# A fused attention and routing layer in fp32: the output projection as three fp32r products, two small jobs moved between engines, and a new order of work on every engine

## The reference, cut to what matters

```python
y   = clip((x * style) @ W.T * dcoef + bias, -256, 256)        # x: [128, 64, 256]
xn  = layernorm(y) * g + b
q   = l2norm(xn @ Wq) * q_scale;  k = l2norm(y @ Wk) * k_scale;  v = y @ Wv    # 16 heads of 64
att = softmax(q k^T * 8 + alibi, causal, 2 null keys) @ v       # within 64 rows
x1  = x + att @ Wout
kx  = modulated_linear(x1);  o = softmax over the heads of kx, mixed;  z = modulated_linear(o)
y2  = z + (small routed network chosen per row by two argmaxes over tile scores of z)
out = x1 + layernorm(y2) * gamma + beta
```

## Time and profile before

| | |
|---|---|
| three timed runs | 1832.64, 1833.00, 1834.09 us; median 1833.0 |
| the profiled execution | 1833.11 us, its span in the trace 1831.3 us |
| busy share of the span | PE 94%, weight loads 79%, DVE 84%, ACT 65%, POOL 64% |
| granted TensorE clock, mean | 0.97 |
| DMA | 93.63 MB moved, 51 GB/s over the span |

### The profile page before, as it was taken

The page is one execution under the profiler, slowest core; times in us unless marked ns, Lnnn a source line. Parts: engine busy times, 40 slices in busy tenths (PEclk is TensorE's granted clock), DMA queues, the critical chain, the costliest instruction groups (busy, mean ns, idle before and its releaser), DMA issues.

```text
span 1831.3 us, 62542 instructions
## 1 busy us (share of the span) xinstructions
PE 1718.0 (94%) x24806; PEld 1439.5 (79%) x24806; DVE 1545.9 (84%) x4182; ACT 1198.5 (65%) x2418; POOL 1173.0 (64%) x903
## 2 busy tenths in 40 slices
PE   4789999999999999999999999999999999999752
PEld 3568888888888888888888888888888888888641
DVE  5567799888989998889989988899899888998744
ACT  2456677777667777776676777676777777667431
POOL 0345557776777677767776777677767776776433
PEclk8899999999999999999999999999999999999875
DMA  4001222222222221222122212221222122212221
GB/s 150 15 9 29 42 49 49 49 55 59 48 46 53 59 49 45 53 59 49 45 56 56 52 42 55 56 52 45 55 54 55 43 52 55 55 47 50 55 54 44
DMA packets 341245, 93.63 MB, mean 51 GB/s; under 512 B 278289, under 2 KB 338097, under 8 KB 341169
## 3 DMA queue, kind: packets, MB, share of 16 engines
q1 hardware_dynamic: 338096, 82.04, 20.6%
q0 software_dynamic: 3072, 10.52, 2.1%
HBM read 58.95 MB, written 33.55 MB: 51 GB/s over the span
## 4 chain that ended last, share of the span: by engine, by line
PE 88%; DVE 5%; ACT 2%; POOL 1%; DMA 1%; issue 1%; SPq 1%; POOLq 0%; ACTq 0%; DVEq 0%
PE pa L442 29%; PE pb L421 7%; PE pa L449 6%; PE ps L645 6%; PE ps L487 6%; PE ps L472 5%; PE ps L479 4%; PE pc L542 4%; PE pc L622 3%; PE pa L421 3%; PE ps L557 3%; PE pb L433 3%; PE ps L489 2%; PE pb L551 2%; PE pb L428 2%; PE pc L568 1%
## 5 line engine op out<-in xcount | busy, mean ns | idle before, releaser
L1131 POOL TENSOR_TENSOR rn<-nrg,mhalf 128x16 f32<-128x16 f32 x64 | 186.6, 2915 | 160.6 <-DVE nrg L1037 160.6
L1117 POOL TENSOR_TENSOR rn<-nrg,mhalf 128x16 f32<-128x16 f32 x64 | 193.2, 3018 | 119.5 <-DVE nrg L970 119.4
L442 PE MATMUL pa<-wv,y 128*128 128x512 f32 x768 | 209.6, 409 | 0.0
L442 PE MATMUL pa<-wq,xnTs 128*128 128x512 f32 x768 | 205.1, 411 | 0.3 <-ACT kcat L703 0.3
L442 PE MATMUL pa<-wk,y 128*128 128x512 f32 x768 | 194.3, 402 | 0.9 <-ACT qn L722 0.9
L442 PEld LDWEIGHTS pa<-wq,xnTs 128*128 128x128 f32 x768 | 139.3, 191 | 51.8 <-issue 23.5
L442 PEld LDWEIGHTS pa<-wk,y 128*128 128x128 f32 x768 | 139.3, 188 | 30.9 <-ACT qn L722 1.7
L1111 POOL TENSOR_TENSOR pr<-pr,rden 128x1056 f32<-128x1056 f32 x64 | 124.7, 1949 | 54.5 <-DVE rden L943 51.8
L442 PEld LDWEIGHTS pa<-wv,y 128*128 128x128 f32 x768 | 135.4, 189 | 23.2
L1006 DVE TENSOR_TENSOR qn<-qn,rn 128x1024 f32<-128x1024 f32 x64 | 112.7, 1762 | 15.6 <-POOL rn L1117 15.0
L1092 POOL TENSOR_TENSOR kn<-kn,rn 128x1024 f32<-128x1024 f32 x64 | 122.0, 1905 | 5.0
(11 more groups left out here) (216 smaller groups left out, 4863.3 us busy)
## 6 DMA issues: line engine op xcount, KB each, us to landing
xT<-in_xT SPq DMA_DIRECT2D x64, 128.0 KB
x<-in_x SPq DMA_DIRECT2D x64, 128.0 KB, 2.1
kxdr<-kxn SPq DMA_DIRECT2D x64, 128.0 KB, 1.7
x1d<-x SPq DMA_DIRECT2D x64, 128.0 KB, 1.8
vm<-kxdr SPq DMA_DIRECT2D x128, 64.0 KB
odr<-o SPq DMA_DIRECT2D x256, 32.0 KB
on<-odr SPq DMA_DIRECT2D x64, 128.0 KB
xb<-x1d SPq DMA_DIRECT2D x64, 128.0 KB, 2.2
```

Source lines behind the costliest of these rows:

```text
L442: last = mm(bank, part(lhs(a_, k)), part(rhs(b_, k)), start=(n == 0), stop=(n == 3 * CK - 1))
L1117: g.tensor_tensor(rn[:, 0, :], nrg[:, 0, :], mhalf[:, :], ALU.pow).then_inc(S("q_rsqrt"), 1)
L1131: g.tensor_tensor(rn[:, 1, :], nrg[:, 1, :], mhalf[:, :], ALU.pow).then_inc(S("k_rsqrt"), 1)
```

## The change

1. Output projection in high and low parts. ScalarE writes the attention output from PSUM as `oH` (fp32r), VectorE writes the rest `oL = PSUM - oH`, and `Wout` is split once into `wout2`. The product is oH x high, oH x low and oL x high: 24 fp32r matmuls of 256 columns in place of 8 plain fp32 ones.
2. The layer norm `xn` of y is applied by ScalarE as scale and shift; GpSimd makes the shift (two more instructions of one column).
3. The guards of the squared norms go from VectorE to GpSimd, each with one small extra instruction ahead (`idle`).
4. The order of the blocks is new on every engine, and the ages differ: TensorE now reaches back 7 tiles (before 9), VectorE 10 (before 11), SyncE 12 (before 11).
5. Some semaphores of the set-up are merged.

```diff
+                    for r in range(HP):
+                        for a in range(2):
+                            mm(ps[:, 2, C:2 * C], part(oH[:, r, :]), part(wout2[:, a, r, :]), start=(r == 0 and a == 0), stop=False)
...
+                    for r in range(HP):
+                        mm(ps[:, 2, C:2 * C], part(oL[:, r, :]), part(wout2[:, 0, r, :]), start=False, stop=False)
...
-                    for r in range(4, HP):
-                        mm(ps[:, 2, C:2 * C], oT[:, r, :], wout[:, r, :], start=False, stop=False)
...
-                    for r in range(4):
-                        mm(ps[:, 2, C:2 * C], oT[:, r, :], wout[:, r, :], start=(r == 0), stop=False)
...
+                    fn(part(oH[:, :, :].rearrange("p r (s l) -> p s r l", s=BT)),
+                       ps[:, 0:2, :].rearrange("p s (r l) -> p s r l", l=L), ACT.Copy).then_inc(S("oT_done"), 1)
...
+                    fn(xn[:, :], pa[:, 2, C:2 * C], ACT.Identity, bias=rs[:, 1:2], scale=rs[:, 0:1]).then_inc(S("xn_done"), 1)
...
+            dve.wait_ge(S("high_parts"), 4)
+            v.tensor_tensor(part(wout2[:, 1, :, :]), wout[:, :, :], wout2[:, 0, :, :], ALU.subtract)
...
+                    v.tensor_tensor(part(oL[:, :, :].rearrange("p r (s l) -> p s r l", s=BT)),
+                                    ps[:, 0:2, :].rearrange("p s (r l) -> p s r l", l=L),
+                                    oH[:, :, :].rearrange("p r (s l) -> p s r l", s=BT), ALU.subtract).then_inc(S("oT_low"), 1)
...
-                    v.tensor_scalar(xn[:, :], pa[:, 2, C:2 * C], mv[:, 0:1], rs[:, 0:1], ALU.subtract, ALU.mult)\
-                        .then_inc(S("xn_done"), 1)
...
-                    v.tensor_scalar(nrg[:, 0, :], nrm[:, 0, :], 1e-24, None, ALU.max).then_inc(S("q_guard"), 1)
...
+                    wait(pool, "k_norm", t2)
+                    g.tensor_tensor(idle[:, 1:2], eps[:, :], eps[:, :], ALU.add)
+                    g.tensor_scalar(nrg[:, 1, :], nrm[:, 1, :], 1e-24, None, ALU.max).then_inc(S("k_guard"), 1)
```

More of the change, by code:

```diff
@@ L323, in pipeline @@
                 step(n * 2 + first + 1, 1)
-            for i in range(last, T + 11):
+            for i in range(last, T + 12):
                 step(i, i % 2)
@@ L365, in step @@
                         .then_inc(D("xT_in", p), 16)
[L366 to L372, removed]
+                if live(i, 9):
+                    if live(i, 11):
+                        wait(sp, "res_done", t11)
+                    wait_dma(sp, "x1_out", t9, 1 - p)
+                    sp.dma_start(xb[:, 1 - p, :], plain(x1d, t9)).then_inc(D("x1_back", 1 - p), 16)
                 if live(i, 5):
@@ L501, in step @@
[L501 to L525, removed]
@@ L545, in step @@
                     last.then_inc(S("mix_scores"), 1)
[L546 to L553, removed]
+                if live(i, 2):
+                    wait(pe, "v1_done", t2)
+                    wait(pe, "qn_done", t2)
+                    four(pa[:, 1, :], qn, 4).then_inc(S("qT1_mm"), 1)
+                    wait(pe, "v0_done", t2)
+                    four(pa[:, 0, :], qn, 0).then_inc(S("qT0_mm"), 1)
@@ L901, in step @@
-                if live(i, 9) or live(i, 10):
-                    if live(i, 10):
-                        wait(dve, "local_exp", t10)
-                    route = links_from(0, t9)
-                    route(v.tensor_scalar(fl[:, :, :], esc[:, :, :], 1.0, None, ALU.add))
-                    route(v.reciprocal(fl[:, :, :], fl[:, :, :]))
-                    route(v.scalar_tensor_tensor(out=over[:, :, :], in0=bc(both(fl), 2, KN), scalar=float(KN - 1),
-                                                 in1=bc(CO["steps"], 1, 2 * NC), op0=ALU.mult, op1=ALU.subtract))
+                t1, t2, t3, t4, t5, t6, t7, t8, t9, t10 = (i - n for n in range(1, 11))
@@ new lines, in step @@
+                if live(i, 3):
+                    wait(dve, "probs", t3)
+                    v.tensor_reduce(den[:, :], heads, AX, ALU.add).then_inc(S("den_done"), 1)
+                    wait(dve, "den_done", t3)
+                    v.reciprocal(rden[:, :], den[:, :]).then_inc(S("rden_done"), 1)
+                if live(i, 1):
+                    v.tensor_tensor(part(y3[:, 1 - p, 1, :, 0:BT, :]), yT[:, :, :, :], y3[:, 1 - p, 0, :, 0:BT, :], ALU.subtract)
+                    v.tensor_tensor(part(y3[:, 1 - p, 1, :, BT, :]), yT[:, :, 0, :], y3[:, 1 - p, 0, :, BT, :],
+                                    ALU.subtract).then_inc(S("yT_low"), 1)
```

748 lines of the change are left out of this document (400 added, 348 removed).

## The result

The changed kernel takes 1949.9 us in the median (four runs, 1936.7 to 1954.9) against 1833.0: the ratio is 1.063, 95% interval 1.057 to 1.068. It is slower, on the side and by the mechanism that the prediction took as the likeliest, and inside its range. The profiled execution is the fastest of the four, 1936.7 us with a span of 1934.9.

What follows compares the result with a forecast made beforehand. TensorE bounded the kernel at 26.06 us a step; VectorE would take over at 27.6. 60 x (27.6 - 26.06) = +92, +2 and -8 on 1833.1 gave 1919 us, own range 1885 to 1965, all cases 1785 to 1965.

Steps and rivals of the forecast that it cites:

- its slack of 1.5 us: VectorE's waits for TensorE in a step of the kernel before: 1.46 us, so VectorE stands 1.5 us behind.
- the third collision: Not in the prediction: GpSimd's `res` falls on VectorE's sum over the hidden units or the next instruction.
- the sum: Per-step work and waits gave a 27.6 us period; over 60 steps +92, set-up +2, pipeline end -8: +86 us.
- the ring: Not in the prediction: TensorE needs 7.9 us from `xm2` towards `om`, VectorE some 20 back; their order sets the period.
- TensorE's side: Output projection: 3.5 us of plain records removed, 24 x 0.13 = 3.1 us added; TensorE's work falls by 0.4 us.
- 256 columns are dear: Rival: 0.216 us per fp32r matmul of the projection, TensorE needs 27.7 us a step, 1930 us; chance 0.04.
- The first collision: Behind `rden`, GpSimd's 1.95 us product makes VectorE's second low part of y wait: 1.8 us lost each step.
- The second collision: GpSimd's scaling of `kn` makes VectorE's high part of y wait 1.0 us (0.7 to 1.9) each step.
- The ends: Outside the steady steps: set-up gains a VectorE subtraction, +2 us; the pipeline, a step shorter at its end, -8.
- the forecast's own range: 1885 to 1965 us, from a period of 27.2 (no waits left) to 28.3 (`kn` costing 1.9).
- The rival without collisions: GpSimd reaches `rden` late and `kn` falls behind the clipping: period 25.4 us, 1788 us; chance 0.36.
- what would show it: Signs in the new profile; the one judged: TensorE has gaps ahead of the transposes of q and of kx.

Runs made afterwards that it cites:

- e5: The changed kernel with the output projection undone: plain fp32 matmuls, no low part on VectorE; 1926.3 us.
- e8: The kernel of e7 with the output projection undone: plain fp32 matmuls, no low part on VectorE; 1856.8 us.
- e7: The kernel of e1 with the statistics of the sum and `xm2` on VectorE moved ahead of the clippings; 1908.4 us.
- e1: The changed kernel with the two subtractions for the low parts of y moved ahead of the softmax sum on VectorE; 1919.1 us.
- e4: The kernel before with the two subtractions for the low parts of y moved directly behind the reciprocal `rden`; 1910.4 us.
- e3: The changed kernel with the edits of e1 and e2 together; 1874.8 us.
- e13: The kernel of e7 with TensorE's program written out for all steps in place of a loop over pairs of steps; 1814.4 us.
- e12: The kernel of e7 without the eight matmuls of `oL` with the high part of wout, so the output lacks that product; 1806.1 us.
- e10: The kernel before with four more one-element matmuls on TensorE in each step, ahead of the output projection; 1898.2 us.
- e11: The kernel of e10 with two in place of four of the one-element matmuls in each step; 1854.7 us.
- e2: The changed kernel with `kn` scaled by GpSimd in one of its 16 heads alone; 1870.5 us.

## Why the prediction was right, and where it was off

- **Which engine bounds.** Right: VectorE took over, its slack of 1.5 us was used up. The size of the period owes something to luck: the terms below that were too small (`kn`, the third collision) and the one that was too large (`oL`) partly cancel. What the sum lacked is the ring: it asked how much work VectorE has in a step, not on which side of `xm2` and `om`. e5 shows that `oL`'s 1.14 us (1.14 measured too), which the sum counted as a loss, cost about 0.1, since TensorE needs that stretch anyway.
- **TensorE's side.** The 24 matmuls of 256 columns in a steady step of the changed kernel (timeline, PE):

```profile
1030.82 2.17 PE L495 MATMUL ps<-wout,oH 128*128 128x256 f32 x16
1032.83 0.38 PE L438 MATMUL pb<-ident,zT 128*128 128x128 f32 x2
...
1033.65 1.19 PE L512 MATMUL ps<-wout,oL 128*128 128x256 f32 x8
1034.77 0.65 PE L514 MATMUL ps<-nullw,pnT 32*64 32x256 f32 x4
```

  From start to the next start they take 2.01 + 1.12 = 3.1 us, 0.13 each, as in the sum; e8's plain ones take 3.65, so that the gain is 0.5 us a step where the sum had 0.4; the periods of e7 and e8 (26.4 and 27.0) agree. "256 columns are dear" is out. The estimate of 2.6 us that the prediction drew from the Trainium skill's figure for a weight load ("TensorE: Matmul & The Clock Gate", "LDWEIGHTS (loading the stationary operand)") is too low; the trace decides.
- **The first collision.** Right in place, instruction and size: -1.8 forecast, 2.04 - 0.28 = 1.76 measured, with GpSimd waiting 2.6 us ahead of `rden` (1.5 to 3 forecast). e1 and e4 show what it is worth: 1.4 less in the changed kernel (0.46 went to `fl`), 1.3 more in the kernel before.
- **The second collision.** Right in cause, off in place and size. Counted from k's norm as there, `kn` asks at +3.6 as forecast, and VectorE comes to `yT` 0.3 us sooner than forecast. But by the prediction's own times the two adding clippings, at about +4.0 and +4.3, already lay inside `kn`'s hold from +3.6 to +5.5. It let them pass without a reason and made only the high part wait, 1.0 us from +4.5. The first clipping starts 0.03 us behind `kn` and is held up for 1.7 (inside the 0.7 to 1.9 given). The high part is next: e1 shows it held up when the clippings come ahead of `kn`. So an operation with one input and per-partition scalars in SBUF is locked out too. The Trainium skill ("GPSIMD Engine Reference", section "8. Key points") counts among those that contend with GpSimd the operations of VectorE in a 2-port perf mode, besides those with two SBUF inputs. That would fit: the one-input high part of 256 columns takes 0.29 us where an operation with two inputs takes 0.42. No trace here names the mode.
- **The third collision** was missed: `res` on `hid` and `junk` in turn, together 0.46 us a step (their means are 422 and 450 ns, before 235 and 175).
- **The sum.** Period 27.6 forecast, 28.2 measured. Between the first and the last softmax sum the profiled execution takes 1756.0 us against 1632.7, +123.3, of which 6.9 are the two stalls; the sum had +92 for this. The ends are -19.7 where the sum had +2 and -8: the first softmax sum comes 8.2 us earlier, and the stretch behind the last is 11.5 us shorter. That the time still falls into the range beside a longer period and the stalls is in part these ends, which is luck. The result is 1950 against 1919. The lower bound of the forecast's own range doesn't follow from its period: 27.2 gives 60 x 1.14 - 6 = +62, 1895 us and not 1885.
- **Missing altogether: the stalls.** They are 7 us of the profiled execution. The median of the timed runs lies 13 us above that execution; four more stalls of 3.4 us would make that up, which is an estimate, since no profile shows such a run. Their granted clock, 0.965 to 0.967 against 0.973, is on the side of more stalls. The prediction counted records, work and waits, but not the length of the program between two jumps.
- **The rival without collisions** gave a period of 25.4 and 1788 us. e3 has 25.6 and takes 1875: its arithmetic was right to 0.2 us a step, and its conclusion wrong by 87 us, because of the stalls. Had VectorE's collisions not happened, the change would still have been slower as it stood. Without stalls and without the two large collisions (e13, `xm2` moved too) it is 1.1% faster than the kernel before. The second forecast of "what would show it", a gap ahead of the transposes of q, is wrong (there is none in the steady step), the gap ahead of kx is right.

## What to carry to other kernels

Before you place an operation of VectorE that reads two SBUF operands, or a `tensor_scalar` on SBUF, ask which GpSimd product its predecessor has just released: 0.3 us of work became 2.0 in each step. Put there what the product doesn't hold up, as `nrm`'s sum in e1 (1.20 us beside the product), and look at what meets the product's end. Ask for a saving on which side of a ring of waits it lies; 1.1 us taken from VectorE where TensorE needed the time anyway was worth 0.1. And when a change adds instructions to a loop, compare the instruction queue's packets with those of before. If they rise and TensorE waits for "issue" at the loop's start, shorten the body (e12) or write it out (e13).

## What was not expected of the hardware

- A loop of TensorE with 16 more matmuls and 16 more loads in a pass of some 775 and 775 stalls at its start, for 1.7 to 5.1 us, in some passes and not in others; with 8 and 8 more it doesn't (e10, e11). Each stall comes with nine packets on the instruction queue, and a pass without a stall has none. With a faster step more passes tend to stall (2 in the changed kernel at 28.2 us a step, 13 to 16 in e1, e3 and e7 at 25.6 to 26.8), but e2 and e10, at 26.6, have 7 and 8. Why some passes escape stays open.
- A stall costs more than TensorE's own wait, because the clock falls beside it: 4.7 to 4.8 us of idle time lengthened a step by 6.8 us in e3 and e7, where TensorE has next to no slack, and by 5.5 in e1. In the changed kernel, where TensorE waits for `xm2` in each step anyway, it was 3.4, with 3.4 us at 1.2 GHz.
- The same program written out reads 3.29 MB of instructions, where e7 with its 13 stalls reads 2.85 and the kernel before 0.90, and doesn't stall (e13).
- Such a kernel is also uneven: four times of e1 spread over 1.1%, of e3 over 0.8%, those of e4 and e13, without stalls, over 0.1%.
